# Vision tower with a top-2 expert layer on one core: a slot table and filler matmuls in place of the scatter, and the first expert product in an order by row height

## What is computed

```python
logits = xf @ Wr + br
gates = jax.nn.softmax(logits, axis=-1)
top_g, top_i = jax.lax.top_k(gates, K)          # K = 2 of E = 8
for e in range(E):
    w_e = jnp.sum(top_g * (top_i == e), axis=-1)
    h = jax.nn.gelu(xf @ W1[e] + b1[e], approximate=False)   # 192 -> 768
    y = h @ W2[e] + b2[e]                                    # 768 -> 192
    out = out + w_e[:, None] * y
```

## Time and profile before

| | us |
|---|---|
| median of 3 runs | 630.85 (627.7 to 631.73) |
| the profiled execution | 634.18 |
| its span | 632.4 |
| first product of the first expert tile starts | 485.81 |
| mean granted TensorE clock | 0.829 of 2.4 GHz |

### The profile page before, as it was taken

How to read it: one execution, slowest core, us unless ns; L and a number is a source line. 1 busy time by engine, 2 the same in 40 slices (tenths; PEclk the granted TensorE clock), 3 DMA queues, 4 the chain that set the end, 5 groups by cost and what they waited for, 6 DMA issues and landing times.

```text
span 632.4 us, 8623 instructions
## 1 busy us (share of the span) xinstructions
PE 512.4 (81%) x3314; PEld 414.0 (65%) x3314; DVE 269.5 (43%) x735; ACT 183.7 (29%) x439; POOL 120.2 (19%) x127
## 2 busy tenths in 40 slices
PE   4899999796967798999999579755503999999992
PEld 4876766695846676877578458754402788777872
DVE  5467545435474745635355666853400011111100
ACT  0222323212323616346452255221100222222120
POOL 2220100011120110111001230117861021221121
PEclk9979569878886969999999879855555599999897
DMA  8800000000290000000050000200113137666742
GB/s 320 205 2 0 1 1 1 2 1 1 66 250 11 0 1 2 2 0 1 1 150 1 1 2 2 76 1 13 24 17 78 37 96 200 168 202 187 219 106 41
DMA packets 23725, 39.29 MB, mean 62 GB/s; under 512 B 6167, under 2 KB 16399, under 8 KB 23474
## 3 DMA queue, kind: packets, MB, share of 16 engines
q1 hardware_dynamic: 16484, 35.40, 19.3%
q0 software_dynamic: 7056, 2.69, 3.4%
q10 hardware_dynamic: 144, 0.64, 0.3%
HBM read 31.51 MB, written 7.91 MB: 62 GB/s over the span
## 4 chain that ended last, share of the span: by engine, by line
PE 64%; DVE 15%; POOL 6%; issue 5%; ACT 5%; DMA 3%; POOLq 0%; SPq 0%; DVEq 0%; ACTq 0%
PE bank L1274 14%; PE bank L1285 6%; PE bank L1231 5%; PE bank L1503 5%; PE bank L1251 5%; PE bank L1209 4%; POOL expert_rows L552 4%; PE bank L1411 4%; PE bank L1455 3%; PE bank L1298 3%; PE bank L1240 3%; PE bank L1470 2%; ACT xn L581 2%; DVE stats L758 2%; PE bank L1352 2%
## 5 line engine op out<-in xcount | busy, mean ns | idle before, releaser
L480 POOL TENSOR_TENSOR rstd<-rstd_tmp,minus_half 101x4 f32<-101x4 f32 x20 | 20.5, 1025 | 333.1 <-DVE rstd_tmp L768 333.1
L1274 PE MATMUL bank<-arena_k,weights 128*128 128x128 f32 (+1 forms) x288 | 68.5, 355 | 0.4 <-issue 0.2
L1274 PEld LDWEIGHTS bank<-arena_k,weights 128*128 128x128 f32 (+1 forms) x288 | 48.4, 210 | 19.9 <-issue 6.5
L1251 PE MATMUL bank<-weights,rep 96*111 96x192 f32 (+1 forms) x320 | 56.8, 327 | 0.0
L1175 DVE TENSOR_SCALAR arena_k<-bank,arena_k 128x192 f32<-128x192 f32 x17 | 7.1, 417 | 113.5 <-PE bank L1285 113.5
L1251 PEld LDWEIGHTS bank<-weights,rep 96*111 96x111 f32 (+1 forms) x320 | 52.2, 175 | 2.2 <-issue 2.1
L560 POOL DMA_INDIRECT rows_out<-arena_k x17 | 26.4, 1551 | 122.6 <-DVE arena_k L1175 112.9
L1231 PE MATMUL bank<-nT,weights 96*96 96x296 f32 (+1 forms) x144 | 42.9, 446 | 3.8 <-DVE nT L783 2.5
L730 ACT ACTIVATE rep<-bank,parameters 128x128 f32<-128x128 f32 x48 | 14.2, 366 | 87.2 <-PE bank L1274 87.2
L552 POOL DMA_INDIRECT expert_rows<-x_rows,spot_row x16 | 35.6, 2223 | 11.5 <-issue 10.6
L1503 PE MATMUL bank<-weights,oT 96*101 96x192 f32 (+1 forms) x144 | 34.9, 412 | 3.0 <-issue 1.8
(11 more groups left out here) (243 smaller groups left out, 891.9 us busy)
## 6 DMA issues: line engine op xcount, KB each, us to landing
weights<-in_w SPq DMA_DIRECT2D x12, 576.0 KB, 4.4
weights<-in_w SPq DMA_DIRECT2D x12, 384.0 KB, 4.5
expert_rows<-blank_row SPq DMA_DIRECT2D x1, 3977.0 KB, 22.3
arena_k<-in_w SPq DMA_DIRECT2D x5, 576.0 KB, 4.2
arena_k<-in_patches SPq DMA_DIRECT2D x4, 606.0 KB, 8.4
weights<-in_w SPq DMA_DIRECT2D x12, 192.0 KB, 5.3
arena_k<-in_w SPq DMA_DIRECT2D x5, 384.0 KB, 4.4
arena_k<-expert_rows SPq DMA_DIRECT2D x17, 97.0 KB, 2.1
```

The costliest lines, as they stand in the source:

```text
L1251: last = mm(o, nrep[q][k][0:96 + k, im], w(n + "_qkv", k, 2 * D, D), start=(k == 0), stop=(k == 1 and n != "B"))
L1274: last = mm(PS[2 * (j % 2) + half][:, TILE * x:TILE * x + TILE], w1b[j % WSETS][0:r, k, 128 * m:128 * m + 128], xT[j % 2][0:r, k], start=( ...
```

## The change

Four things are changed together.

1. **A slot table.** The normed tokens are stored once to `rows_x` in HBM (by SyncE, as soon as they are normed). For each token choice VectorE makes a row of 128 zeros and one 1 at its lane (`hit`), GpSimd a row of 41 columns for each of three values, with the token number, the gate and a 1 in the column of its tile (`entry`). 16 matmuls add these up to one table, 128 lanes x 41 tiles, of token numbers and gates (job `table`). GpSimd gathers each tile's rows by it (`gather`), and adds results by it. 16 scatters, the copies into `x_rows` and the row loads of SyncE are gone; `plan_tiles` runs before the `eb` sums.
2. **Fillers.** `keep_busy(j, n)` issues n matmuls of the 128 x 128 identity into the bank of job j, before TensorE waits for something. There are 198 of them before the last tile starts.
3. **First expert product.** Six matmuls over 128 rows, then six over 64 rows, whose operands stand on partitions 0 to 63 for even and 64 to 127 for odd blocks, with the results of even and odd blocks in two banks. VectorE copies the last 64 features to both halves (three copies a tile in place of two), the weights come in three DMAs in place of two, and ScalarE starts when all six blocks are done.
4. **Queues of the tiles.** SyncE no longer waits for the adds. GpSimd's list is, for each tile: wait for the result, wait for the add before, add, gather the rows of tile j+6.

```diff
+IDLE_T = {("B", 1): 11, ("D", 1): 8, ("F", 1): 25, ("G", 1): 9, ("H", 0): 10, ("H", 1): 12}
+IDLE_R = 19
+IDLE_O = {("B", 0): 12, ("C", 0): 12, ("C", 1): 15, ("G", 1): 14}
+IDLE_CUM, IDLE_SLOT, IDLE_ROWS = 9, 6, 8
...
-        return [("cum", q)]
+        return [("cum", q)] + [("table",)] * q
...
+            def keep_busy(j, n):
+                b, k = where[j]
+                if k:
+                    pe.wait_ge(bank_read[b], k)
+                for _ in range(n):
+                    mm(PS[b][:, 0:128], ident, ident, start=True, stop=True)
```

SyncE:

```diff
+                for i in range(2):
+                    r = slice(64 * i, 64 * i + 64)
+                    sp.dma_start(w1b[b][r, 1].rearrange("p (x i n) -> p i x n", i=2, n=128)[:, i],
+                                 w1[e][r, 1].rearrange("p (x i n) -> p i x n", i=2, n=128)[:, i]).then_inc(w1_loaded[b], 16)
...
-            sp.wait_ge(scattered, 16 * TOPK * PAIRS)
-            for j in range(XBUFS):
-                load_x(slice(j * REGION, j * REGION + TILE), j)
+            for q in octs:
+                sp.wait_ge(*xn_ready.at(("H", q)))
+                store_rows(rows_x, xn, q, x_stored)
...
-                    sp.wait_ge(added, 16 * j + 16)
-                    load_x(slice(row, row + TILE) if n < NE else bass.ds(row, TILE), n % XBUFS)
```

GpSimd:

```diff
-                    link(g.tensor_copy(xa[0:ROWS, a, 1, 0:D], xa[0:ROWS, a, 0, 0:D]))
...
+                    link(g.tensor_tensor(col[:, :, 2], past_begin[0:ROWS, :, 0:COLS], past_begin[0:ROWS, :, 1:], ALU.subtract))
+                    which = token[0:ROWS, P8 * q:P8 * q + P8].unsqueeze(2).unsqueeze(3).broadcast_to([ROWS, P8, TOPK, COLS])
+                    link(g.tensor_tensor(col[:, :, 0].rearrange("p (c k) x -> p c k x", k=TOPK), col[:, :, 2].rearrange("p (c k) x -> p c k x", k=TOPK), which, ALU.mult))
                     pool.wait_ge(*spots_ready.at(q))
-                    for r in range(P8 * q, P8 * q + P8):
-                        for k in range(TOPK):
-                            g.indirect_dma_start(slots, bass.IndirectOffsetOnAxis(spot_row[0:ROWS, r, k:k + 1], 0), xa[0:ROWS, r, k, :], None,
-                                                 bounds_check=XROWS - 1, oob_is_err=False).then_inc(scattered, 16)
+                    g.tensor_tensor(col[:, :, 1], col[:, :, 2], gate, ALU.mult).then_inc(*entries_ready.inc(q))
...
+            pool.wait_ge(slots_ready, 1)
+            pool.wait_ge(x_stored, 16 * 4 * len(octs))
+            for j in range(XBUFS):
+                gather(j)
+            pool.wait_ge(plan_ready, 2)
+            for j in range(SPARE):
+                col = pool.value_load(tile_of[0:1, 1, j:j + 1], min_val=0, max_val=COLS - 1)
+                g.tensor_copy(tile_row[:, j:j + 1], slot_row[:, bass.ds(col, 1)]).then_inc(spares_ready, 1)
+                g.tensor_copy(tile_gate[:, j:j + 1], slot_gate[:, bass.ds(col, 1)]).then_inc(spares_ready, 1)
...
+                g.indirect_dma_start(rows_out, bass.IndirectOffsetOnAxis(at, 0), yb[j % 3], None,
                                      bounds_check=T + TILE - 1, compute_op=ALU.add).then_inc(added, 16)
+                if j + XBUFS < TILES:
+                    pool.wait_ge(xT_filled, j + 1)
+                    gather(j + XBUFS)
```

VectorE, in `route_spots` (n is 8, so `past_begin` is 101 x 336 and a half's `hit` 101 x 1024; the two `spot_row` writes go) and behind it (`slot_tables` is three operations on at most 41 columns):

```diff
+                v.tensor_tensor(past_begin[0:ROWS], spots.unsqueeze(2).broadcast_to([ROWS, n, COLS + 1]),
+                                begins[0:ROWS].unsqueeze(1).broadcast_to([ROWS, n, COLS + 1]), ALU.is_ge).then_inc(*begins_ready.inc(q))
...
+                link(v.tensor_reduce(depth[0:ROWS], past_begin[0:ROWS], AX.X, ALU.add))
+                link(v.scalar_tensor_tensor(depth[0:ROWS], depth[0:ROWS], -float(TILE), spots, ALU.mult, ALU.add))
+                v.tensor_tensor(hit[0:ROWS, n * q:n * q + n], depth[0:ROWS].unsqueeze(2).broadcast_to([ROWS, n, TILE]),
+                                lane[0:ROWS].unsqueeze(1).broadcast_to([ROWS, n, TILE]), ALU.is_equal).then_inc(*hits_ready.inc(q))
...
+            slot_tables()
+            plan_tiles()
             for c in range(PAIRS // 2):
 
                 add_bank(("eb", c), h[0:ROWS, 2 * c:2 * c + 2], h[0:ROWS, 2 * c:2 * c + 2])
-            plan_tiles()
```

TensorE:

```diff
+                    if q:
+                        keep_busy(("table",), IDLE_SLOT)
+                        ps = start_job(("table",))
+                        n_ = PAIRS * TOPK
+                        for x in range(n_):
+                            if x % (n_ // 2) == 0:
+                                pe.wait_ge(*hits_ready.at(x // (n_ // 2)))
+                                pe.wait_ge(*entries_ready.at(x // (n_ // 2)))
+                            last = mm(ps[:, 0:3 * COLS], hit[0:ROWS, x], entry[0:ROWS, x].rearrange("p w c -> p (w c)"), start=(x == 0), stop=(x == n_ - 1))
...
+            for _ in range(IDLE_ROWS):
+                mm(PS[6][:, 0:128], ident, ident, start=True, stop=True)
             turn_x(0)
...
-                        for k, r in enumerate((128, D - 128)):
-                            last = mm(PS[2 * (j % 2) + half][:, TILE * x:TILE * x + TILE], w1b[j % WSETS][0:r, k, 128 * m:128 * m + 128], xT[j % 2][0:r, k],
-                                      start=(k == 0), stop=(k == 1))
...
+                for m in range(MT):
+                    part(m, slice(0, 128), 0, m < 2, False)
+                for m in range(MT):
+                    part(m, slice(64 * (m % 2), 64 * (m % 2) + 64), 1, False, m >= MT - 2).then_inc(fc1_done, 1)
```

More of the change, by code:

```diff
@@ L907, in route_spots @@
             def route_spots(q):
-                j, a, m = ("cum", q), slice(P8 * q, P8 * q + P8), P8 * NE
-                spot, last, share = (taken[0:ROWS, x].rearrange("p (c e) -> p c e", e=NE) for x in range(3))
-                high, both, low = (spots[0:ROWS, x, a] for x in range(3))
+                j, a, m, n = ("cum", q), slice(P8 * q, P8 * q + P8), P8 * NE, TOPK * P8
+                at, last, part = (taken[0:ROWS, x].rearrange("p (c e) -> p c e", e=NE) for x in range(3))
+                low, high = (spot[0:ROWS, a, x] for x in range(TOPK))
+                both = total[0:ROWS]
                 dve.wait_ge(*filled(j))
@@ L914, in route_spots @@
                 dve.wait_ge(*evacuated(j))
-                mark(v.tensor_reduce(high, spot, AX.X, ALU.max))
-                link(v.tensor_reduce(both, spot, AX.X, ALU.add))
-                mark(v.tensor_tensor(low, both, high, ALU.subtract))
-                mark(v.tensor_scalar(spot_row[0:ROWS, a, 1], high, nowhere[0:ROWS], -1.0, ALU.add, ALU.add))
-                link(v.tensor_tensor(last, spot, high.unsqueeze(2).broadcast_to([ROWS, P8, NE]), ALU.is_equal))
-                mark(v.tensor_scalar(spot_row[0:ROWS, a, 0], low, nowhere[0:ROWS], -1.0, ALU.add, ALU.add))
@@ L921, in route_spots @@
[L921 to L925 removed]
+                mark(v.tensor_reduce(high, at, AX.X, ALU.max))
+                link(v.tensor_reduce(both, at, AX.X, ALU.add))
@@ new lines, in route_spots @@
+                link(v.tensor_tensor(low, both, high, ALU.subtract))
+                if q != octs[0]:
+                    dve.wait_ge(*entries_ready.at(octs[0]))
+                spots = spot[0:ROWS, a].rearrange("p c k -> p (c k)")
+                v.tensor_tensor(past_begin[0:ROWS], spots.unsqueeze(2).broadcast_to([ROWS, n, COLS + 1]),
+                                begins[0:ROWS].unsqueeze(1).broadcast_to([ROWS, n, COLS + 1]), ALU.is_ge).then_inc(*begins_ready.inc(q))
+                mark(v.tensor_tensor(last, at, high.unsqueeze(2).broadcast_to([ROWS, P8, NE]), ALU.is_equal))
@@ new lines, in route_spots @@
+                dve.wait_ge(*disp_ready.at(("H", q)))
+                settle()
+                link(v.tensor_tensor(part, last, disp[0:ROWS, a], ALU.mult))
+                mark(v.tensor_reduce(share[0:ROWS, a, 1], part, AX.X, ALU.add))
+                link(v.tensor_tensor(last, disp[0:ROWS, a], part, ALU.subtract))
+                v.tensor_reduce(share[0:ROWS, a, 0], last, AX.X, ALU.add).then_inc(*spots_ready.inc(q))
+                dve.wait_ge(*begins_ready.at(q))
+                link(v.tensor_reduce(depth[0:ROWS], past_begin[0:ROWS], AX.X, ALU.add))
@@ new lines, in route_spots, with slot_tables @@
+                link(v.scalar_tensor_tensor(depth[0:ROWS], depth[0:ROWS], -float(TILE), spots, ALU.mult, ALU.add))
+                v.tensor_tensor(hit[0:ROWS, n * q:n * q + n], depth[0:ROWS].unsqueeze(2).broadcast_to([ROWS, n, TILE]),
+                                lane[0:ROWS].unsqueeze(1).broadcast_to([ROWS, n, TILE]), ALU.is_equal).then_inc(*hits_ready.inc(q))
+                dve.wait_ge(*hits_ready.at(q))
+            def slot_tables():
+                j = ("table",)
+                dve.wait_ge(*filled(j))
+                row, gate, busy = (bank(j)[:, COLS * x:COLS * x + COLS] for x in range(3))
+                link(v.tensor_scalar(unused[:], busy, 1.0, spare_row[:], ALU.subtract, ALU.mult))
+                v.tensor_tensor(slot_row[:], row, unused[:], ALU.add).then_inc(slots_ready, 1)
```

(2 more changed lines are left out.)

164 lines of the change are left out of this document (93 added, 71 removed).

## The result

| | before | after |
|---|---|---|
| median | 629.28 us (625.57 to 631.73, 4 runs) | 566.06 us (563.06 to 569.22, 4 runs) |
| ratio to before | | 0.9001 (0.893 to 0.9071, 95%) |
| profiled execution, its span | 634.18, 632.4 us | 566.39, 564.2 us |
| mean granted clock | 0.829 | 0.916 |

The kernel is 10% faster.

A forecast was written before the change was run, and what follows sets the result against it. TensorE, often at 1.2 GHz, was taken to bound the kernel, with a wait for scatters before the tiles. 632.4 - 13 - 7 - 26 - 45 = 541.4 us of span, so 540 us; range 518 to 572.

The forecast's parts named there:

- The tiles' bound: Expert tiles: GpSimd would be late next, its adds waiting for the landing of the add before, not for the product.
- I take 5.4 while weights load: Expert tiles: period between GpSimd's adds, 5.4 us beside weight loads, from bounds of 5.0 and 8.5; last six at 4.3.
- part 4: First expert product to the end: 101 us where it was 146.6, so -45 us.
- Rival (a): Expert tiles: adds dearer through bunched weights and gathers in the same queue; period 7 us, time 556 us; chance 0.22.
- Rival (d): Expert tiles: adds and gathers go strictly one after another; period 11 us, 637 us of summed time; chance 0.03.
- TensorE's tile: TensorE's work per expert tile: 5.0 us (4.8 to 5.6) where it was 7.17, with the first product at 2.66.
- Rival (b): Expert tiles: TensorE is the bound because the halves don't overlap; tile 5.6 us, time 545 us; chance 0.12.
- The first add: Start of the tiles: GpSimd's first add starts 14 us (9 to 18) after the first expert product.
- The slot table: Counts to first expert product: 15 us where it was 40.9, so -26 us (-20 to -28).
- Fillers before the counts: Routing, from the expert logits to the second half's counts: fillers gain 7 us (2 to 11).
- Fillers in the tower: Tower, up to the first expert logits: fillers raise the clock, -13 us, between +5 and -20.
- Rival (c): Tower, routing and first tiles: fillers leave the clock at 1.2 GHz, first 22 us of tiles cold; 574 us; chance 0.10.

The follow-up runs named there:

- e2: The changed kernel with the first product's 128-row and 64-row matmuls in turn again, short ones still on alternate halves: 591.11 us, ratio 0.9354.
- e9: The changed kernel without fillers and with the first product's heights in turn, so the slot table and its queues alone: 609.86 us, ratio 0.9673.
- e3: The changed kernel without the weight loads of tiles 3 to 16, which reuse the first three sets: 544.12 us, no ratio.
- e4: The changed kernel without the eleven gathers between the adds; later tiles reuse the first six tiles' rows: 552.39 us, no ratio.
- e10: The changed kernel with two tables of sums and all six short matmuls of a tile on partitions 0 to 63: 555.75 us, ratio 0.8778.
- e5: The changed kernel with adds of odd tiles going to a second table in HBM, both summed at the end: 548.1 us, ratio 0.8651.
- e1: The changed kernel with no filler matmul anywhere: 575.59 us, ratio 0.914.
- e6: The kernel before with the fillers alone, all but those of the table: 626.06 us, ratio 0.988.
- e7: The kernel before with the new first expert product alone (order by height, halves, three loads, three copies): 605.63 us, ratio 0.9538.

## Why the prediction was right or wrong

**The tiles' bound: right, its price wrong.** That GpSimd would be late next, waiting for the landing of the add before, held. The step that failed is "I take 5.4 while weights load": the period was 6.63 us, and sixteen periods took 95.2 us where the sum had 10 x 5.4 + 6 x 4.3 = 79.8. With the first add 5.4 us earlier than priced and the end as priced, this is the 10 us by which part 4 missed. I took 5.4 from between 4.3 and 8.5, close to the quiet landings, because the median of before was 4.0. That median is over all 17 adds. For those from 523.7 to 592.1 us alone, where weights load, the kernel before has:

```profile
DMA to landing us min/median/max: 3.5/5.8/7.7
```

So the landing under weights was 5.8 us before the change, as it is after it. With the 0.8 us that lie between a landing and the next add (4.28 less 3.47) that gives a period of 6.6, the one measured. The tiles' length has little to do with it: e2 and e9, at 7.17 us a tile, have a median of 5.2 us over all their adds, the kernel after 5.3. e3 shows that the weights do it (3.5 over all without them). What changed is that TensorE's tile of 7.17 us used to be longer than 6.6 and hid the landings, and 4.58 is not. Rival (a) named dearer adds with a period of 7, and the measured one lies nearer to that than to 5.4. Of its two reasons e3 shows that the weights count, though not that their bunching does; the second, the gathers in the same queue, is worth at most the 0.5 us of e4. Rival (d), adds and gathers strictly one after another, is out.

The Trainium skill (DMA: Bandwidth & Descriptors, SWDGE vs HWDGE vs iDMA) has the engines alternate between the two kinds of queues. An add that lands in 5.8 us beside the weights and in 3.6 without them is slowed by them even so; whether it took turns with them or stood behind them no run here tells.

**TensorE's tile: right, and a little cheaper.** 5.0 us was priced, 4.58 measured. A change of height was priced at 0.16 and costs 0.19. A record of 128 columns was priced at 0.12 and costs 0.10. The short records were priced at 0.075 and take 0.05 to 0.055: two run at a time, as e10 shows. The 0.075 came from layer A, whose records change halves only every eighth. Rival (b), no overlap, is out. None of this moved the time, since the tile lay below the period; in e5 it is the period.

**The first add: too dear.** It was priced at 14 us behind the first product and came at 8.6. GpSimd's gathers take 1.08 us each, not 1.55, and the nine numbers with their copies about 3 us, not 9. From 454.3 us on it waited for TensorE's result. It helped by 5.4 us.

**The slot table: nearly right.** 18.5 us against 15. Slot numbers stood at 8.1 us (442.23), not 6.7: VectorE's work took 5.4 us and not 4.2 (below). The eight fillers took 3.75 us, not 1.8. I had priced them at full clock, but the clock stood at 0.50 from 445.8 to 452.6, and here they stand behind the last wait, where nothing hides them. The order of the paths was as predicted: the `eb` sums of VectorE, at 12.7 us, came last and set the start. But this part has two lengths, by the clock. The kernel after, e3 and e10 have 2.06 us for the table's matmuls in the chain and 18.5 us from counts to first product; e2, e4 and e5 have 22.5, and this is the chain of e5:

```profile
438.74 3.78 PE bank L1459 x16
...
444.44 5.37 PE bank L1622 x16
...
450.72 3.76 PE bank L1627 x16
```

The table's matmuls run at half the clock, and with them the products of `eb` (the 5.37), so TensorE is later than VectorE's sums and the fillers come on top. e9 has the slow table too (3.78) but no fillers, and takes 19.0 us (446.79 to 465.74). So with the slow table the eight fillers behind the last wait cost 3.5 us. With the table at full clock the part is 0.4 shorter than without any filler, though the eight take their 3.75 us there too. What decides between the two clocks the runs don't tell.

**Fillers before the counts: wrong.** 7 us were predicted, 1.9 came (2.1 against e1, whose part is 31.8 us). The clock stayed at 0.50 from 408.2 to 415.1 and from 421.9 to 432.1, and in the second place the fillers themselves became the last thing waited for: 3.93 us in the chain, priced at nothing because "the counts are waited for". The wait before them was shorter than nine fillers at 1.2 GHz: the pick they stood in front of was there at 431.07, and they ended at 432.49, so of the 3.93 us some 1.4 are their cost.

**Fillers in the tower: wrong size.** 13 us were predicted. The trace shows 8.8, but that is not the fillers' worth: e1 has the first logits as early without them (404.61 against 404.52), e9 10.5 us later, and e6 with them 4.1 earlier than before. By medians all fillers together, those before the counts included, give 9 (e1) and 8 us (e6). The step that failed is scaling 22.6 us of slow TensorE time by the chain's 64% in every stretch alike. By the comparison under e6 the stretch 184 to 202, which that prices at 3.9, gave nothing, 358 to 372 at 2.6 nothing either, and 154 to 164 at 2.6 gave 0.5, though the clock rose in all three; 222 to 232 gave more than its 2.8. The place with the 11 fillers, counted as nought, cost 2.8. And the tower's length moves by itself: with the table and the same fillers it was 392.8 us in e4 and 404.5 in the kernel after, without fillers 404.6 and 415.0. A term of 13 us with such a spread could not be read from one trace. Rival (c), that the fillers leave the clock as it is, did not hold for the clock; for the time it was half right. It also had the first 22 us of the tiles cold without fillers; the order of the first product, not the fillers, warmed them (e9).

**The parts alone** give 20.6 (e9) + 29.1 (e7) + 7.6 (e6) = 57 us, together 63; within the widths of the measurements the parts add up. The profiled executions are less even: behind the first product the order is worth 23.4 us on the kernel before (146.6 to 123.2 in e7, one of the slower executions) and 29.4 on the one with the table (e9 to e1). Why was not tried.

## What to carry to other kernels

When a change speeds up the engine that hides a transfer, price the transfer in the stretch of the trace where the other loads run, not at its median over the whole run (5.8 and 4.0 us here). This chain of accumulating transfers to one target was bound by their landing, not by bandwidth, and a second target with one sum at the end took it away (e5: 22 us net, with 4 spent at the end). Fillers must be shorter than the wait at the low clock's price, and they want a measured time as their proof: a higher granted clock alone says little. Nor is a tower of one execution such a proof: the same program moved by 10 to 12 us.

## What the runs showed of the hardware that I had not expected

**VectorE was held by GpSimd, operation by operation.** VectorE and GpSimd of the kernel after, in order of time:

```profile
435.62 0.72 DVE L962 TENSOR_TENSOR taken<-taken,disp 101x32 f32<-101x32 f32 x1
436.37 0.19 DVE L963 TENSOR_REDUCE share<-taken 101x4 f32<-101x32 f32 x1
436.47 0.68 DVE L964 TENSOR_TENSOR taken<-disp,taken 101x32 f32<-101x32 f32 x1
```
```profile
435.56 0.73 POOL L565 TENSOR_TENSOR vblk<-past_begin 101x328 f32<-101x328 f32 x1 [13.91 <-DVE past_begin L957]
436.37 0.74 POOL L567 TENSOR_TENSOR vblk<-vblk,token 101x328 f32<-101x328 f32 x1
```

L962 and L964 have 32 elements and two operands; alone, in the kernel before, the same operations took 0.18 us. Each began beside a GpSimd operation and ended within 0.05 us of its end (436.34 and 436.29; 437.15 and 437.11). L963, with one operand, took its usual 0.19 us beside L567. The Trainium skill (SBUF — State Buffer, SBUF: two separate sides) calls the port pair that both share an exclusive lock, which a VectorE operation with two SBUF inputs needs and which blocks it until the GpSimd operation is done; this trace agrees. With L968, also with two inputs, which took 0.46 us beside the third GpSimd operation and 0.17 in the first half, it cost about 1.3 us in the path, and my sum of 4.2 us lacked it.

**The same program, 10.4 us apart by its clock alone** (e1 and e9, above), and 11.7 us between e4 and the kernel after.

**A busy TensorE that stayed at 1.2 GHz for 15 to 22 us** at the start of the tiles, in every kernel with the heights in turn (before, e2, e6, e9), and in none with the order by height (e9, above).

**A place that stays open.** In the kernel before, layer A's matmuls at 41 us took 3.00 us and the clock was at 0.50 from 41.0 to 47.8; in the change they take 1.76 us, and the clock is 1.00 from 40 to 50 us. TensorE's rows, before and after:

```profile
41.00 3.00 PE L1337 MATMUL bank<-arena_k,qT 96*64 96x102 f32 x32
```
```profile
40.08 1.76 PE L1412 MATMUL bank<-arena_k,qT 96*64 96x102 f32 x32
```

No filler stands before this place. The change is 0.9 us ahead when it comes there and 3.6 behind it, so the place accounts for 2.7 of the 8.8 us in the tower. It was so in every run with the slot table and in none with the scatter (before, e6, e7); why was not tried.
